# Projection of an inverted-residual block: z2 laid out by pair, quarter and partition, and two of four channel tiles multiplied as two fp16 parts

## What is computed

```python
planes = w1.shape[0]                                                     # 576
out = relu(batchnorm(conv(x, ternarize(w1)), g1, b1))                    # 1x1, 96 -> 576
out = relu(batchnorm(conv(out, ternarize(w2), pad=1, groups=planes), g2, b2))   # 3x3 depthwise; its result before batchnorm is "z2"
out = batchnorm(conv(out, ternarize(w3)), g3, b3)                        # 1x1, 576 -> 96; before batchnorm it is "z3"
return out + x
```

## Time and profile before

| | |
|---|---|
| median of 3 runs | 5873.81 us (5856.16 to 5875.26) |
| the profiled execution | 5871.17 us, of which its span is 5869.3 |
| busy, share of the span | PE 92%, DVE 62%, ACT 58%, POOL 29%; DMA queue of SyncE 63.7% |
| convolution stage, some 300 to 2050 us | PE 1663.6 of the 1700 us from 300 to 2000; DMA share 0.66, 162 GB/s |
| projection stage, 2056 to 2880 us | PE 807.4 of 824 us; ACT 550.5, DVE 250.5, POOL 0; DMA share 1.01, 326 GB/s |
| second layer, from 2880 us | PE 2714.0 of 2989 us, granted clock 0.88; DMA share 0.56, 153 GB/s |

### The profile page before, as it was taken

One profiled execution on the slowest core, in us unless ns is written; L12 is line 12 of the kernel. 1 busy time (PEld: TensorE's weight loads), 2 busy tenths in 40 slices (PEclk: granted clock), 3 DMA queues, 4 the chain that ended last, 5 costly groups with the idle time before them and its releaser, 6 DMA issues. The chain is left out here.

```text
span 5869.3 us, 145952 instructions
## 1 busy us (share of the span) xinstructions
PE 5416.5 (92%) x59604; PEld 3550.5 (60%) x59604; DVE 3610.0 (62%) x6670; ACT 3419.5 (58%) x5674; POOL 1704.1 (29%) x964
## 2 busy tenths in 40 slices
PE   4979999999999799999679999999999999999996
PEld 4956666666666444444257667667667667666663
DVE  1036666666666723333327777777777777777775
ACT  2445555555555366676446666666666666666652
POOL 0037777777777400000011111111111111111110
PEclk9989999999999899999869888999988999989986
DMA  3646766666666499999745655665665665665551
GB/s 84 157 117 159 174 164 170 170 170 168 167 173 159 117 326 326 333 340 334 235 142 145 165 162 153 167 163 154 165 163 153 166 170 157 164 168 155 161 136 44
DMA packets 553171, 1041.24 MB, mean 177 GB/s; under 512 B 178512, under 2 KB 347280, under 8 KB 535888
## 3 DMA queue, kind: packets, MB, share of 16 engines
q1 hardware_dynamic: 552512, 1031.93, 63.7%
HBM read 552.39 MB, written 478.94 MB: 176 GB/s over the span
## 5 line engine op out<-in xcount | busy, mean ns | idle before, releaser
L718 POOL TENSOR_TENSOR hlo<-h,hhi 128x1682 f16<-128x1682 f32 x288 | 977.2, 3393 | 447.8 <-DVE hhi L749 447.8
L733 DVE BATCH_NORM_STATS2 stats<-z 128x6 f32<-128x392 f32 x1152 | 597.3, 560 | 517.6 <-ACT z L670 507.7
L1514 POOL TENSOR_TENSOR y<-zin,x_tok 96x448 f32<-96x448 f32 x224 | 263.2, 1176 | 2199.5 <-ACT zin L1470 2198.0
L680 ACT ACTIVATE h<-c1ps,s 128x1512 f32<-128x1512 f32 x288 | 465.1, 1615 | 696.7 <-PE c1ps L596 696.7
L888 PE MATMUL pps<-z2m,w3T 128*96 128x392 f32 x2048 | 709.7, 499 | 19.0 <-ACT z2m L865 18.9
L617 PE MATMUL dwps<-hhi,taps 64*64 64x392 f16 x13824 | 689.0, 330 | 2.5 <-issue 2.4
L617 PE MATMUL dwps<-hlo,taps 64*64 64x392 f16 x13824 | 681.4, 327 | 1.4 <-issue 1.3
L865 ACT ACTIVATE z2m<-z2m,s 128x784 f32<-128x784 f32 x512 | 490.9, 1029 | 262.3 <-DMA z2m<-z_scratch 262.2
L1522 POOL TENSOR_TENSOR onat<-tb,o 96x448 f32<-96x448 f32 x224 | 238.6, 1065 | 1150.8 <-DVE o L1581 1150.8
L888 PEld LDWEIGHTS pps<-z2m,w3T 128*96 128x96 f32 x2048 | 322.8, 163 | 396.5 <-issue 343.1
L617 PEld LDWEIGHTS dwps<-hlo,taps 64*64 64x64 f16 x13824 | 406.1, 106 | 179.3 <-issue 2.8
(11 more groups left out here) (218 smaller groups left out, 10038.4 us busy)
## 6 DMA issues: line engine op xcount, KB each, us to landing
z_scratch<-z SPq DMA_DIRECT2D x1152, 196.0 KB, 3.3
z2m<-z_scratch SPq DMA_DIRECT2D x128, 1568.0 KB, 20.1
a_scratch<-a SPq DMA_DIRECT2D x224, 384.0 KB, 2.8
bt<-a_scratch SPq DMA_DIRECT2D x96, 672.0 KB, 8.8
c_scratch<-cc SPq DMA_DIRECT2D x128, 336.0 KB, 4.7
d<-c_scratch SPq DMA_DIRECT2D x128, 336.0 KB, 4.7
xa<-in_x_dram SPq DMA_DIRECT2D x32, 1176.0 KB, 7.3
xin<-in_x_dram SPq DMA_DIRECT2D x32, 1176.0 KB, 8.7
```

What stands on the lines that cost most here:

```text
L680: nc.scalar.activation(to, src, ACT.Relu, bias=s1[:, 1, u:u + 1], scale=s1[:, 0, u:u + 1]).then_inc(h_ready, 1)
L718: nc.gpsimd.tensor_tensor(to, h, hi, ALU.subtract).then_inc(lo_ready, 1)
L733: nc.vector.bn_stats(stats[:, i, v, at:at + 6], z2[:, v % 3, g, r, :]).then_inc(s_stat, 1)
```

## The change

1. z2 in HBM gets the shape (pair, quarter, partition, slot, 784), with nine slots: 0 to 3 the tiles of image 0, 4 to 7 those of image 1, 8 the last 64 channels of both. A quarter of a pair is then two loads of 128 partitions, with one run of 4 or 5 slots (12544 or 15680 bytes) for each partition, in place of four loads with runs of 3136 bytes. `z2m` takes the same shape in SBUF; `z2t` is gone.
2. Tiles 2 and 3 of each image are multiplied as an fp16 high part and an fp16 rest, with w3's two tiles in fp16 (its values -1, 0, 1 are exact). ACT does tiles 2 and 3 first. DVE casts them to the high part, POOL subtracts it from the f32 value, and PE does four fp16 matmuls for each chunk and image (two tiles, two parts) in place of two f32 ones. Tiles 0, 1 and the last 64 channels stay f32, and the split matmuls come last in a chunk.
3. DVE's cast for image c % 2 of the next quarter stands ahead of the copies of chunk c. The split buffer `hl` holds two quarters.
4. The stores of z3's halves move: half 0 is issued after the load of quarter 2 of the next pair, half 1 after the load of quarter 0 of the pair after that.

```diff
-    z2_d = nc.dram_tensor("z2_scratch", (NB, UN, 2, 32, 4, 2 * QN), F32, kind="Internal").ap()
+    z2_d = nc.dram_tensor("z2_scratch", (NP, 4, 128, 9, 2 * QN), F32, kind="Internal").ap()
...
+                m, u = v // UN, v % UN
+                p, slot = (64 * m, 8) if u == UN - 1 else (64 * (u % 2), 4 * m + u // 2)
                 for q in range(4):
-                    dst = z2_d[2 * i + v // UN, v % UN, :, :, q, :].rearrange("g c x -> c g x")
+                    dst = z2_d[i, q, p:p + 64, slot, :].rearrange("(g c) x -> c g x", g=2)
...
-            z2m = sb("z2m", [128, 2, 4, TOK], ctx=st)
-            z2t = sb("z2t", [128, TOK], ctx=st)
+            z2m = sb("z2m", [128, 4, 9, QC], ctx=st)
+            hl = sb("h2_split", [128, 2, 2, 2, 2, QC], F16, ctx=st)
+            w3h = sb("w3h", [128, 2, C], F16, ctx=st)
...
             def load_quarter(sp, i, q):
-                cols = slice(q * QC, q * QC + QC)
+                for m, slots in enumerate((slice(0, 4), slice(4, 9))):
+                    sp.dma_start(z2m[:, q, slots, :], z2_d[i, q, :, slots, :]).then_inc(ldm[q][m], 16)
+
+            def store_half(sp, i, h):
+                sp.wait_ge(z3_ready, (i * 2 + h + 1) * 8)
                 for m in range(2):
-                    src = z2_d[2 * i + m].rearrange("u g c y x -> (u g c) (y x)")[:, cols]
-                    sp.dma_start(z2m[:, m, :, cols], src[0:512, :].rearrange("(t p) x -> p t x", p=128)
-                                 ).then_inc(ldm[q][m], 16)
-                    sp.dma_start(z2t[64 * m:64 * m + 64, cols], src[512:576, :]).then_inc(ldt[q], 16)
...
+                    if q == 2:
+                        store_half(sp, i, 0)
+                    if q == 0 and i > 0:
+                        store_half(sp, i - 1, 1)
...
+            @block.gpsimd
+            def _(pool):
+                for n in range(4 * NP):
+                    for m in range(2):
+                        pool.wait_ge(hi_ready, 2 * n + m + 1)
+                        wait_count(pool, p_full, 4 * n - 4)
+                        h32, hi, lo = split_views(n, m)
+                        nc.gpsimd.tensor_tensor(lo, h32, hi, ALU.subtract).then_inc(lo_ready, 1)
...
-                        for t in range(4):
-                            nc.tensor.matmul(banks[m], w3T[:, t, :], z2m[:, m, t, cols], start=(t == 0), stop=False)
...
+                        for t in range(2):
+                            nc.tensor.matmul(banks[m], w3T[:, t, :], z2m[:, c // 2, 4 * m + t, cols],
+                                             start=(t == 0), stop=False)
...
+                    for m in range(2):
+                        if first:
+                            pe.wait_ge(hi_ready, 2 * n + m + 1)
+                            pe.wait_ge(lo_ready, 2 * n + m + 1)
+                        for t in range(2):
+                            for k in range(2):
+                                ins = nc.tensor.matmul(banks[m], w3h[:, t, :], hl[:, n % 2, k, m, t, cols],
+                                                       start=False, stop=(t == 1 and k == 1))
+                        ins.then_inc(p_full, 1)
...
+            def split_vector(dve, n, m):
+                dve.wait_ge(h2_ready, n * 9 + 4 * m + 2)
+                wait_count(dve, p_full, 4 * n - 4)
+                h32, hi, lo = split_views(n, m)
+                nc.vector.tensor_copy(hi, h32).then_inc(hi_ready, 1)
...
+                    if i * 4 + c // 2 + 1 < 4 * NP:
+                        split_vector(dve, i * 4 + c // 2 + 1, c % 2)
```

More of the change, by code:

```diff
@@ L817, in build @@
             ldm = [[sem(f"z2_loaded{q}_{m}", st) for m in range(2)] for q in range(4)]
-            ldt = [sem(f"z2_last_loaded{q}", st) for q in range(4)]
             h2_ready = sem("h2_ready", st)
+            w3_ready = sem("w3_halved", st)
+            hi_ready = sem("h2_hi", st)
+            lo_ready = sem("h2_lo", st)
             p_full = sem("conv3_done", st)
@@ L829, in load_quarter, with project_dma @@
             def load_quarter(sp, i, q):
[L830 removed]
+                for m, slots in enumerate((slice(0, 4), slice(4, 9))):
+                    sp.dma_start(z2m[:, q, slots, :], z2_d[i, q, :, slots, :]).then_inc(ldm[q][m], 16)
+            def store_half(sp, i, h):
+                sp.wait_ge(z3_ready, (i * 2 + h + 1) * 8)
                 for m in range(2):
[L832 to L837 removed]
+                    to = z3_d[2 * i + m].rearrange("c (a h x) -> h c a x", a=2, h=2)[h]
+                    sp.dma_start(to, z3[:, h, m, :, :]).then_inc(stz[h], 16)
+            def project_dma(sp, i):
                 for q in range(4):
[L839 removed]
+                    if i < NP - 1:
                         sp.wait_ge(p_full, (i * 4 + q + 1) * 4)
                         load_quarter(sp, i + 1, q)
[L842 to L846, removed]
+                    if q == 2:
+                        store_half(sp, i, 0)
+                    if q == 0 and i > 0:
+                        store_half(sp, i - 1, 1)
             @block.sync
@@ L851, in _ @@
                     load_quarter(sp, 0, q)
-                for i in range(0, NP - 1):
-                    project_dma(sp, i, True)
-                project_dma(sp, NP - 1, False)
+                for i in range(NP):
+                    project_dma(sp, i)
+                store_half(sp, NP - 1, 1)
                 for h in range(2):
@@ L859, in project_scalar @@
                 for q in range(4):
-                    cols = slice(q * QC, q * QC + QC)
                     for m in range(2):
                         act.wait_ge(ldm[q][m], i * 16 + 16)
-                        for t in range(4):
-                            v = z2m[:, m, t, cols]
+                        for t in (2, 3, 0, 1):
+                            v = z2m[:, q, 4 * m + t, :]
                             nc.scalar.activation(v, v, ACT.Relu, bias=s2[:, 1, t:t + 1], scale=s2[:, 0, t:t + 1]
                                                  ).then_inc(h2_ready, 1)
-                    act.wait_ge(ldt[q], i * 32 + 32)
-                    nc.scalar.activation(z2t[:, cols], z2t[:, cols], ACT.Relu, bias=s2[:, 1, 4:5], scale=s2[:, 0, 4:5]
-                                         ).then_inc(h2_ready, 1)
+                    v = z2m[:, q, 8, :]
+                    nc.scalar.activation(v, v, ACT.Relu, bias=s2[:, 1, 4:5], scale=s2[:, 0, 4:5]).then_inc(h2_ready, 1)
             @block.scalar
@@ L876, in _, with split_views @@
                 nc.scalar.activation(gtmp[0][:, :], gtmp[0][:, :], ACT.Sqrt).then_inc(s_std, 1)
+            def split_views(n, m):
+                h32 = z2m[:, n % 4, 4 * m + 2:4 * m + 4, :].rearrange("p t x -> p (t x)")
+                hi, lo = (hl[:, n % 2, k, m, :, :].rearrange("p t x -> p (t x)") for k in range(2))
+                return h32, hi, lo
+            @block.gpsimd
[6 more added lines that the diff above has]
+                        nc.gpsimd.tensor_tensor(lo, h32, hi, ALU.subtract).then_inc(lo_ready, 1)
@@ L891, in project_tensor @@
+                    if first:
+                        pe.wait_ge(h2_ready, n * 9 + 9)
                     for m in range(2):
                         half = slice(64 * m, 64 * m + 64)
-                        nc.tensor.matmul(banks[m], w3T[half, 4, :], z2t[half, cols], start=False, stop=True
-                                         ).then_inc(p_full, 1)
+                        nc.tensor.matmul(banks[m], w3T[half, 4, :], z2m[half, c // 2, 8, cols], start=False, stop=False)
+                    for m in range(2):
+                        if first:
+                            pe.wait_ge(hi_ready, 2 * n + m + 1)
[5 more added lines that the diff above has]
+                        ins.then_inc(p_full, 1)
@@ L896, in _ @@
             @block.tensor
             def _(pe):
-                project_tensor(pe, 0)
-                for i in range(1, NP):
+                pe.wait_ge(w3_ready, 1)
+                for i in range(NP):
                     project_tensor(pe, i)
+            def split_vector(dve, n, m):
[3 more added lines that the diff above has]
+                nc.vector.tensor_copy(hi, h32).then_inc(hi_ready, 1)
@@ L923, in link @@
                     dve.wait_ge(s_ch, chain[0])
-                project_vector(dve, 0)
-                for i in range(1, NP):
+                nc.vector.tensor_copy(w3h[:, :, :], w3T[:, 2:4, :]).then_inc(w3_ready, 1)
+                for m in range(2):
+                    split_vector(dve, 0, m)
+                for i in range(NP):
                     project_vector(dve, i)
```

10 lines of the change are left out of this document (3 added, 7 removed).

## The result

| | before | changed |
|---|---|---|
| median, first comparison | 5865.6 us (4 runs) | 5711.6 us (4 runs) |
| ratio | | 0.9732 (95% interval 0.9700 to 0.9763) |
| the same in a second comparison | 5865.8 us | 5716.6 us, ratio 0.9736 (0.9710 to 0.9761) |
| profiled execution | 5871.2 us | 5686.4 us |
| projection stage in the profile, first to last matmul | 2067.1 to 2878.9 | 2068.2 to 2727.6 |

The account below looks back on a forecast made before the run. PE (12.54 us per quarter) and DMA (12.66) both bound the projection; afterwards DMA at 10.7 would. 64 x (12.66 - 10.7) = -125 us, plus 3, 2 and 3, gives 5754 us; own range 5725 to 5785, wide 5710 to 5825.

Parts of the forecast that it names:

- Two equal bounds before: Projection stage before the change: PE needs 12.54 us per quarter and DMA 12.66, so PE's saving alone is worth nothing.
- PE after the change: Projection matmuls: 4.91 us per chunk, 5.0 with changes between forms, thus 10.0 us per quarter; high end 11.7.
- Transfers: Projection DMA after the change: loads 8.65 us plus store 2.06, 10.7 us per quarter, the bound by 7%.
- The store's share: z3 store's part of a quarter's DMA time, taken as 2.06 us and kept after the change; ends 1.45 and 2.56.
- rival 1: Projection: stores vanish among the loads, DMA falls to 9.9 us per quarter, PE binds at 10.0 to 10.1; 5715 us, chance 0.22.
- Rival 2: Projection: mixing reads and writes, or something behind SBUF, caps the rate; 11.6 us per quarter, 5808 us; chance 0.13.
- Rival 3: Projection: the loop through z3 store, DVE copy, cast, POOL subtraction and PE binds at 13.3 us per quarter; 5911 us, chance 0.10.
- friction: Projection stage: 3 us added to the sum for two bounds only 7% apart.
- DVE and POOL hidden: Projection per quarter: DVE 5.8 us with casts of 0.95 each, POOL 6.3 with subtractions of 3.16 each, all hidden.
- Clock: PE in the projection: idle stops too short to lower its clock; under 0.9 would prove this wrong.
- Convolution: Stage ahead of the projection: moved z2 addresses cost nothing at DMA share 0.66; it ends within 5 us of 2056.
- The sum: Whole kernel: 64 quarters save 125 us, 8 us come back for pipe, start and friction: -117, 5754 us.

Follow-up runs that it names:

- e1: The changed kernel with z2's old layout and loads put back, so only the split matmuls stay: 5871.4 us, ratio 1.0012 to the kernel before.
- e2: The changed kernel with all matmuls back in f32, so only the new layout and loads stay: 5849.6 us, ratio 0.9976 to the kernel before.
- f3: e2 with most projection activations and matmuls removed and the old layout and loads put back, stores kept: 12.45 us per quarter, 331 GB/s.
- f4: f3 with all z3 stores moved behind the last quarter, so old-form loads run alone: 11.68 us per quarter, 306 GB/s.
- f1: e2 with most projection activations and matmuls removed, so new-form loads and stores are the only bound: 9.90 us per quarter, 423 GB/s.
- e3: The changed kernel with z3's stores back at their old places, after the loads of quarters 1 and 3: 5698.2 us, ratio 0.9719; again 5695.3, 0.9714.

## Why the prediction was right and wrong, point by point

- **Two equal bounds before: right** (e1, e2, f3).
- **PE after the change: right.** 4.93 us per chunk against 4.91 to 5.0. Eight fp16 matmuls take 2406.33 - 2404.96 = 1.37 us against 1.35; their weight loads are hidden. PE's idle time was 0.3 us per quarter (18.7/64), not 0.7.
- **Transfers: the mechanism right, the size wrong; this is the step that failed.** "The store's share is 12.66 - 10.6 = 2.06 us" took 341 GB/s for the steady rate of the loads of before, which is 306 (f4), and then carried the share over to another form of loads. Loads 8.65 was 8.47, the store 2.06 was 1.43: 9.90 instead of 10.7 us per quarter, 51 us over 64 quarters. I called the 2.06 my weakest number; its low end of 1.45 was the truth. What I should have seen: the store's 292 GB/s on the margin was already more than the 235 of its form alone, so it wasn't a property of the store; rival 1 had said so.
- **Rival 1 (stores vanish, 5715 us) is what came**, at 0.22: both bounds at 9.9 us. What it says of the rate stands: f1 moves loads and stores at 423 GB/s, loads alone at 428. Its reason (96 partitions leave part of the path free) was not tried, and its sign "PE without gaps" did not come: PE was busy 507.7 of 520 us. That its time is within 4 us is partly luck: it had PE at 10.0 to 10.1 us and 8 us of losses, where PE needed 9.86 and the store loop took the rest.
- **Rival 2 (a cap on the mixture) fell.** 414 to 423 GB/s of reads and writes together; the Trainium skill's 358 GB/s of HBM per core ("DMA: Bandwidth & Descriptors", Specifications) does not bind a core that runs alone here.
- **Rival 3 (the store loop) was there, in a small form.** I had judged that it would drain itself, and mostly it does: the middle of the stage runs at 10.2 us per quarter, not 13. But two quarters after the first took 15.8 and 13.9 us, with the stops of 4.09 and 2.23 us behind a late store, and on average it takes some 0.25 us of each, which the 3 us of friction in the sum (0.05 per quarter) didn't hold.

```profile
2131.24 1.34 PE L919 MATMUL pps<-h_split,w3h 128*96 128x392 f16 x4 [4.09 <-POOL h_split L894]
```

- **DVE and POOL hidden: right; DVE's cast mis-sized.** POOL's subtraction took 3164 ns against 3.16 us. DVE's casts took 955 ns at best and 1.68 us on average, not 0.95; with the store at its old place half of them took 977 ns or less (e3).
- **Clock: right in the main**, 1.00 in the middle of the stage. "Stops too short to lower its clock" was wrong for the two longest: behind the 2.23 us it was 0.50, and behind the 4.09 us too (0.50 from 2132 to 2134). In e1, where PE is busy 85% with stops of up to 7 us, it fell to 0.90; where PE has a fifth of its matmuls (f1 to f4), to between 0.63 and 0.70.
- **Convolution: right.** The first load of the next stage was issued at 2057.9 against 2056.2, the DMA share ahead of it is 0.66 as before.
- **The sum.** 64 x (12.68 - 10.30) = 152 us instead of 117. The errors were -51 (transfers) and, the other way, +15 or so (store loop).

## To carry to other kernels

Where PE and DMA are both near 100% busy, measure each by itself before costing an edit: one of them relieved alone gave 0% and 0.24%, both together 2.7%. In transfers, count partitions first: 11% of the loaded bytes in 64-partition loads cost 2.5 of 12.4 us, while runs four to five times longer were worth 0.33. And look at what is queued behind a wait on its engine when work is added there: a cast put behind a copy that waits for a store brings that store's landing onto PE's path.

## What the hardware showed that was not expected

- **The rate of a mixture isn't a sum of shares.** Between windows 2076 to 2086 and 2150 to 2760 of f4 the same loads fell from 349 to 306 GB/s, with no stores between them; with stores between them (f3) the mixture moved at 331. For these loads a rate read from the first tens of us of a stage isn't the steady rate; why it falls is not shown.
- **DVE's f32 to fp16 cast and POOL's subtraction don't run at the same time.** POOL worked from 2400.65 to 2403.82; the cast that started at 2402.85 took 1.80 us, ending 0.83 us after POOL had ended, though alone (2413.56) it takes 0.95. So it was with all 84 casts of the stage that began while POOL was at work: each ended 0.83 to 0.84 us after POOL's instruction. The casts' spread (first line below: least, median and most in ns) fits, and so does e3's, where few casts meet a subtraction (last line); POOL's 3155 to 3177 ns doesn't move. DVE's copies out of PSUM beside POOL keep their 0.55 us.

```profile
L933 DVE CAST h_split<-z2m x128: 955/1804/2267, 2066.3 to 2714.4; 128x1568 f16<-128x1568 f32 x128
...
L894 POOL TENSOR_TENSOR h_split<-z2m,h_split x128: 3155/3164/3177, 2067.3 to 2715.4; 128x1568 f16<-128x1568 f32 x128
...
L930 DVE CAST h_split<-z2m x128: 951/977/1305, 2063.7 to 2696.7; 128x1568 f16<-128x1568 f32 x128
```
